# An attention block's opening on one core: the order of its first projections, loads and moments

## The reference

```python
xn = layernorm(x)                                   # no scale, no shift, eps 1e-5
kqv = xn @ Wqkv + bqkv                              # 768 columns: q, k, v
scores = einsum('bsnh,btnh->bnst', k, q) / 4
scores = triu(scores) + -10000.0 * tril(ones, k=-1)
attn = softmax(scores, axis=2)                      # over s: down the columns
out = einsum('bnkq,bknh->bqnh', attn, v).reshape(b, s, 256) @ Wo + bo
xq = fp8(clip(xn / in_scale, -448, 448)) * in_scale
return x + out + einsum('bsi,oi->bso', xq, weight * weight_scale)
```

## Time and profile before

| | |
|---|---|
| median of 3 runs | 200.75 us (199.69 to 200.75) |
| the profiled execution | 200.16 us, of which the span is 198.1 us |
| TensorE busy in the span | 175.9 us (89%) |
| VectorE | 161.9 us (82%) |
| GpSimd | 122.8 us (62%) |
| ScalarE | 98.3 us (50%) |
| TensorE's granted clock, mean | 0.955 of full |

### The profile page before, as it was taken

One profiled execution on the slowest core, in us unless ns is written; L12 is line 12 of the kernel. 1 busy time (PEld: TensorE's weight loads), 2 busy tenths in 40 slices (PEclk: granted clock), 3 DMA queues, 4 the chain that ended last, 5 costly groups with the idle time before them and its releaser, 6 DMA issues.

```text
span 198.1 us, 4702 instructions
## 1 busy us (share of the span) xinstructions
PE 175.9 (89%) x1677; PEld 137.6 (69%) x1677; DVE 161.9 (82%) x344; ACT 98.3 (50%) x169; POOL 122.8 (62%) x245
## 2 busy tenths in 40 slices
PE   4597648399989999999999999999999987999992
PEld 4476446278667878787878787878787866776661
DVE  2889989986988899889988998899889987891441
ACT  2614230156546753774377447644664464549410
POOL 7720704415996599459945994599459956666600
PEclk9969966759999999999999999999999999999999
DMA  5799999702530371137113541362126210001003
GB/s 168 180 345 184 234 190 232 132 0 72 144 110 3 95 203 35 55 92 196 45 56 87 135 109 58 87 175 72 56 77 173 81 53 2 6 1 58 0 3 106
DMA packets 23673, 20.35 MB, mean 103 GB/s; under 512 B 2547, under 2 KB 23395, under 8 KB 23651
## 3 DMA queue, kind: packets, MB, share of 16 engines
q1 hardware_dynamic: 23651, 20.06, 40.6%
HBM read 3.48 MB, written 2.10 MB: 28 GB/s over the span
## 4 chain that ended last, share of the span: by engine, by line
PE 73%; DMA 9%; DVE 5%; SPq 4%; POOL 3%; ACT 2%; issue 2%; ACTq 0%
PE pso L1002 8%; PE bankB L1027 8%; PE ps L977 8%; PE bankA L1089 6%; PE bankB L1035 5%; PE bankA L1027 5%; DMA k_stack<-k_parts 4%; SPq L358 4%; PE pso L1008 4%; PE ps L954 3%; PE ps L956 3%; DMA q_stack<-max_rows 3%; PE ps L949 3%; PE ps L982 3%; PE bankB L1056 2%; PE bankA L1074 2%
## 5 line engine op out<-in xcount | busy, mean ns | idle before, releaser
L462 POOL TENSOR_SCALAR_AFFINE_SELECT probs<-probs 128x256 f32<-128x256 f32 x128 | 54.5, 455 | 40.2 <-ACT probs L532 40.0
L743 DVE TENSOR_REDUCE row_max<-ps 128x4 f32<-128x1024 f32 (+1 forms) x48 | 58.2, 1216 | 10.4 <-PE ps L956 9.6
L532 ACT ACTIVATE probs<-ps 128x1024 f32<-128x1024 f32 x48 | 48.9, 1023 | 29.9 <-PE ps L977 23.7
L954 PE MATMUL ps<-k_stack,q_stack 96*128 96x128 bf16 x128 | 19.4, 229 | 2.0 <-DVE row_max L743 2.0
L977 PE MATMUL ps<-q_stack,k_stack 99*128 99x256 bf16 x128 | 20.0, 282 | 0.6 <-DMA q_stack<-max_rows 0.6
L956 PE MATMUL ps<-k_stack,q_stack 125*128 125x128 bf16 x128 | 19.4, 228 | 0.0
L1027 PE MATMUL bankB<-xT,wqk_sb 128*128 128x256 f32 x64 | 17.6, 422 | 1.4 <-ACT xT L582 1.4
L1002 PE MATMUL pso<-probs,v_sb 128*32 128x256 f32 x256 | 17.5, 386 | 0.0
L556 ACT ACTIVATE o_raw<-pso 128x512 f32<-128x512 f32 x16 | 9.6, 597 | 15.9 <-PE pso L1008 15.9
L949 PE MATMUL ps<-k_stack,q_stack 125*128 125x128 bf16 x128 | 11.1, 236 | 6.7 <-DMA k_stack<-k_parts 3.9
L472 POOL TENSOR_TENSOR x_sum<-x_clip,x_big 128x256 f32<-128x256 f32 x16 | 11.3, 723 | 7.3 <-DVE x_big L732 7.3
(11 more groups left out here) (130 smaller groups left out, 347.7 us busy)
## 6 DMA issues: line engine op xcount, KB each, us to landing
q_stack<-q_parts SPq DMA_DIRECT2D x48, 128.0 KB
k_stack<-k_parts SPq DMA_DIRECT2D x48, 128.0 KB
out_dram<-y SPq DMA_DIRECT2D x8, 256.0 KB, 2.1
x_all<-in_L_attn_x_dram SPq DMA_DIRECT2D x1, 1536.0 KB, 8.8
k_stack<-fixed_k SPq DMA_DIRECT2D x3, 256.0 KB
q_stack<-fixed_q SPq DMA_DIRECT2D x3, 256.0 KB
x_all<-in_L_attn_x_dram SPq DMA_DIRECT2D x2, 256.0 KB, 2.8
wqkv_sb<-in_L_attn_Wqkv_dram SPq DMA_DIRECT2D x1, 512.0 KB, 3.8
```

The lines of the kernel that those rows point to most:

```text
L462: ins = pool.affine_select(out=v[:, lo:lo + 2], in_=v[:, lo:lo + 2], compare_op=ALU.is_ge, fill=0.0, base=0, pattern=[[0, 2], [1, P]], cha ...
L532: act.activation(probs[:, i, :], ps[:], ACT.Exp, scale=SCALE).then_inc(exp_done, 1)
L743: dve.tensor_reduce(dst, src, AX_X, ALU.max).then_inc(max_done, 1)
L954: pe.matmul(ps[:, h * S:h * S + P], q_stack[0:PROD, b % STACKS, hh, P:S], k_stack[0:PROD, b % STACKS, hh, 0:P], start=True, stop=True)
```

## The change

1. **Loads.** x comes in four groups: batch 0, batch 1, batches 2 and 3, batches 4 to 7. The last group, `bo` and `wo` are issued behind stack 0's pieces.
2. **Fixed rows of stack 1.** No DMA writes them: ScalarE copies q's (four copies, two on either side of xT of batch 1), GpSimd copies k's (four copies, behind its split of batch 1). TensorE waits for both ahead of phase 1 of batch 1, and `stack_full` counts two DMAs fewer for that stack.
3. **ScalarE's order.** Root 1 is taken behind both first parts of batch 0 instead of ahead of them. In step FIRST the copy of the maxima's rows comes first, then the moments of tiles 10 to 15, root 3, and only then the floor's exponential.
4. **VectorE's order.** Ones are filled into v here instead of on GpSimd. Batch 1's root and normalising go behind q's split; moments and variances of group 2 and the clipping of batch 0's x come ahead of batch 1's rests, its magnitude between them. The fp8 weight, the copy of v's bias, the row numbers and masked keys move in between the first maxima. The moments of two tiles and the variances of group 3 (tiles 8 to 15, six of them with ScalarE's sums) end step FIRST; their reciprocal root is in step 1.
5. **TensorE's order.** The transposes of v's bias and of the fp8 weight move from behind v's product to behind the second block of phase 1, the bias product from behind the second to behind the fourth. The warm-up is 13 products instead of 18 transposes.

```diff
-        WARM_UP = 18
+        WARM_UP = 13
-        X_GROUPS = ((0, TB), (TB, 2 * TB), (2 * TB, B * TB))
+        X_GROUPS = ((0, TB), (TB, 2 * TB), (2 * TB, 4 * TB), (4 * TB, B * TB))
@@ sync
             load_x(2)
-            sp.dma_start(bo_all[:], bo.partition_broadcast(P)).then_inc(proj_landed, 16)
-            sp.dma_start(wo_sb[:], wo.rearrange("(k p) n -> p k n", p=P)).then_inc(proj_landed, 16)
...
             to_stack(0)
-            fixed_in_stack(1)
+            sp.dma_start(bo_all[:], bo.partition_broadcast(P)).then_inc(proj_landed, 16)
+            sp.dma_start(wo_sb[:], wo.rearrange("(k p) n -> p k n", p=P)).then_inc(proj_landed, 16)
+            load_x(3)
             to_stack(1)
@@ gpsimd
-            pool.memset(v_sb[:], 1.0).then_inc(v_ones_ready, 1)
...
+            pool.wait_ge(split_ready, 4)
+            for h in range(0, H, 4):
+                ins = pool.tensor_copy(k_stack[ROW_MAX:ROW_MAX + FIXED_ROWS, 1, h:h + 4],
+                                       fixed_k[:].rearrange("r t p -> r (t p)").unsqueeze(1).to_broadcast([FIXED_ROWS, 4, S]))
+            ins.then_inc(fixed_k_copied, 1)
+            pool.wait_ge(fixed_k_copied, 1)
             round_x(0, 0)
@@ scalar
+            def copy_fixed_q(lo, hi):
+                for h in range(lo, hi, 4):
+                    ins = act.activation(q_stack[ROW_MAX:ROW_MAX + FIXED_ROWS, 1, h:h + 4],
+                                         fixed_q[:].rearrange("r t p -> r (t p)").unsqueeze(1).to_broadcast([FIXED_ROWS, 4, S]),
+                                         ACT.Copy)
+                return ins
...
+            def moments():
+                act.wait_ge(x_landed[3], 16)
+                for t in range(*ACT_TILES):
+                    ins = act.activation(act_out[:, t - ACT_TILES[0]], x_all[:, t, :], ACT.Copy, scale=-1.0 / D,
+                                         accum_out=act_mean[:, t:t + 1])
+                ins.then_inc(act_means, 1)
+                act.wait_ge(act_means, 1)
+                for t in range(*ACT_TILES):
+                    ins = act.activation(act_out[:, t - ACT_TILES[0]], x_all[:, t, :], ACT.Square, bias=act_mean[:, t:t + 1],
+                                         accum_out=act_sum[:, t:t + 1])
+                ins.then_inc(act_squares, 1)
...
-                if st.has(1):
+                if st.like == FIRST:
+                    rows_out(0, 0, "B")
+                    moments()
+                    square_roots(3)
+                    floor_out(0, 0, 0)
+                elif st.has(1):
                     max_out(n + 1, 1 - p, 0, "B")
...
-            for b in range(2):
-                xT_out(b, b)
-                if b == 0:
-                    square_roots(1)
-                    act.wait_ge(bqk_col_ready, 1)
-                part1(b, b, "q", "B")
-                part1(b, b, "k", "A")
+            xT_out(0, 0)
+            act.wait_ge(bqk_col_ready, 1)
+            part1(0, 0, "q", "B")
+            part1(0, 0, "k", "A")
+            square_roots(1)
+            act.wait_ge(const_ready, 2)
+            copy_fixed_q(0, HALF)
+            xT_out(1, 1)
+            copy_fixed_q(HALF, H).then_inc(fixed_q_copied, 1)
+            part1(1, 1, "q", "B")
+            part1(1, 1, "k", "A")
@@ vector, opening (new order)
+            dve.memset(v_sb[:], 1.0).then_inc(v_ones_ready, 1)
...
+            inverse_std(0)
+            normalise(0, 0)
...
+            link(moments(*X_GROUPS[1]))
+            variances(1)
...
             rest1(0, 0, "q", "B")
             split(dve, 0, 0, "q")
+            inverse_std(1)
+            normalise(1, 1)
             rest1(0, 0, "k", "A")
             split(dve, 0, 0, "k")
             dve.wait_ge(x_landed[2], 16)
-            moments(at, at + 5)
+            link(moments(*X_GROUPS[2]))
+            variances(2)
+            clip_x(0, 0)
             rest1(1, 1, "q", "B")
-            moments(at + 5, at + 8)
+            magnitude_x(0, 0)
             rest1(1, 1, "k", "A")
@@ vector, step FIRST
                     maxima(st, n + 1, 0)
+                if st.like == FIRST:
+                    fp8_weight()
...
                 if st.like == FIRST:
-                    inverse_std(2)
+                    dve.wait_ge(x_landed[3], 16)
+                    link(moments(X_GROUPS[3][0], ACT_TILES[0]))
                     normalise(2, 0)
+                    variances(3)
@@ tensor
             for _ in range(WARM_UP):
-                pe.transpose(ps1[:, 0:P], ident[:], ident[:])
+                pe.matmul(ps1[:, 0:P], ident[:], ident[:], start=True, stop=True)
...
                         if st.like == FIRST and i == 1:
+                            transpose_weights()
+                        if st.like == FIRST and i == 3:
                             bias_product()
```

More of the change, by code:

```diff
@@ L53 @@
 PARTS = 3
+ACT_TILES = (5 * TB, B * TB)
 Q_ROWS = (0, 0, 1, 0, 1, 2)
@@ L235, in build @@
         bank = {"A": psum("bankA", [P, 512]), "B": psum("bankB", [P, 512])}
-        x_landed = [sem(f"x{g}_landed") for g in range(3)]
+        x_landed = [sem(f"x{g}_landed") for g in range(4)]
         w_landed, bqk_landed, ffn_landed = sem("w_landed"), sem("bqk_landed"), sem("ffn_landed")
@@ L511, in _ @@
                 split(pool, 1, 1, qk)
+            pool.wait_ge(split_ready, 4)
[4 more added lines that the diff above has]
+            pool.wait_ge(fixed_k_copied, 1)
             round_x(0, 0)
             pool.wait_ge(out_bias_ready, 1)
-            for g in range(3):
-                pool.wait_ge(x_landed[g], 16)
+            pool.wait_ge(x_landed[0], 16)
+            pool.wait_ge(x_landed[1], 16)
             residual(0)
@@ L571, in max_out, with rows_out @@
                                scale=SCALE).then_inc(e_ready, 1)
+            def rows_out(b, half, bk):
+                c = 2 * b + half
                 act.wait_ge(max_mm, c + 1)
@@ L576, in max_out @@
                                ACT.Copy).then_inc(max_rows_ready, 1)
+            def max_out(b, par, half, bk):
+                floor_out(b, par, half)
+                rows_out(b, half, bk)
+            def moments():
[9 more added lines that the diff above has]
+                ins.then_inc(act_squares, 1)
             def xT_out(b, par):
@@ L669, in moments, with aggregate, from_act @@
                 return ins
+            def aggregate(lo, hi):
+                for t in range(lo, hi):
+                    ins = dve.bn_aggr(mean_var[:, t, :], stats[:, t, :])
+                return ins
+            def from_act(lo, hi):
+                dve.wait_ge(act_squares, 1)
+                dve.tensor_scalar(mean_var[:, lo:hi, 0], act_mean[:, lo:hi], -1.0, None, ALU.mult)
+                link(dve.tensor_scalar(mean_var[:, lo:hi, 1], act_sum[:, lo:hi], 1.0 / D, None, ALU.mult))
             def variances(g):
                 lo, hi = X_GROUPS[g]
-                for t in range(lo, hi):
-                    ins = dve.bn_aggr(mean_var[:, t, :], stats[:, t, :])
-                link(ins)
+                if g < 3:
+                    link(aggregate(lo, hi))
+                else:
+                    link(aggregate(lo, ACT_TILES[0]))
+                    from_act(*ACT_TILES)
                 dve.tensor_scalar(var_eps[:, lo:hi], mean_var[:, lo:hi, 1], EPS, None, ALU.add).then_inc(init_dve, 1)
@@ L842, in run @@
                     negate_and_split(n + 1, 0)
+                if st.like == FIRST:
+                    dve.wait_ge(w8_mm, 1)
+                    dve.tensor_copy(w8T[:], pso[:, 1, 1].bitcast(BF16).rearrange("p (k o) -> p k o", k=KT)).then_inc(w8T_ready, 1)
+                    link(dve.tensor_reduce(row_number[:], later[:], AX_X, ALU.add))
+                    for t in range(TB):
+                        ins = dve.tensor_scalar(masked_keys[:, t:t + 1], row_number[:], -1.0, float(S - 1 - P * t), ALU.mult, ALU.add)
+                    link(ins)
                 if st.has(-1):
@@ L897, in _ @@
             dve.wait_ge(x_landed[2], 16)
-            moments(at, at + 5)
+            link(moments(*X_GROUPS[2]))
+            variances(2)
+            clip_x(0, 0)
             rest1(1, 1, "q", "B")
-            moments(at + 5, at + 8)
+            magnitude_x(0, 0)
             rest1(1, 1, "k", "A")
-            fp8_weight()
-            dve.wait_ge(bias_mm, 1)
-            dve.tensor_copy(bv_T[:], pso[:, 0, 0].rearrange("p (k m) -> p k m", k=KT)).then_inc(bv_T_ready, 1)
-            link(moments(at + 8, last))
-            variances(2)
             dve.wait_ge(const_ready, CONSTS)
-            link(dve.tensor_reduce(row_number[:], later[:], AX_X, ALU.add))
-            for t in range(TB):
-                ins = dve.tensor_scalar(masked_keys[:, t:t + 1], row_number[:], -1.0, float(S - 1 - P * t), ALU.mult, ALU.add)
-            link(ins)
             dve.wait_ge(floor_ready, 1)
-            clip_x(0, 0)
             all_steps(dve, run)
@@ L1101, in transpose_max_early, with transpose_weights @@
                 mm.then_inc(max_mm, 1)
```

(18 more changed lines are left out.)

47 lines of the change are left out of this document (27 added, 20 removed).

## The result

The changed kernel takes 205.68 us (median of 4 runs, 204.74 to 205.76), the kernel before 200.74 us beside it (199.69 to 200.75): a ratio of 1.0197, 95% interval 1.0145 to 1.0248. It is slower by 4.9 us, outside the range.

A forecast was written before the change was run, and what follows sets the result against it. The opening, before 58 us, was taken as the bound: q at half clock, DMA backlog, VectorE's maxima, ScalarE's exponential. Gains and additions nearly cancel: 200.16 + 0.1 = 200.3, or 200.8 on the median's base; 200.4 given, range 198.2 to 203.3.

The forecast's parts named there:

- Part 1: Warm-up, q and k of batch 0: 13 products keep the clock up, so q's products end at 11.4 instead of 13.1.
- Part 2: Batch 0's stack: without the 4 us DMA backlog, issues end at 20.1 and it lands at 22.5 instead of 27.6.
- Part 3: Batch 1's normalising and products, v of batch 0: first maximum at 25.5 against 28.78, a gain of 3.3 us.
- Part 4: VectorE between the maxima: additions lengthen its full line by 2.9 us, bounds 2.2 and 3.8; step 0's first maximum at 39.7.
- Part 5: ScalarE's last root and table load: first large exponential 0.6 us later, at 41.4; batch 2's q products at 43.7, +0.1 us.
- rival D: ScalarE's sums come later than VectorE asks for them: +1.5 us, 201.9; chance 0.08.
- the five cases: The prediction's outcomes for the whole time: 200.4 (chance 0.38), 198.8 (0.29), 202.4 (0.20), 201.9 (0.08), 201.7 (0.05).
- B: Faster: batch 1's products at full clock, VectorE's additions only 2.2 us; 198.8, down to 197.8; chance 0.29.
- C: Slower: clock falls before batch 0's q products all the same; first maximum later than 26.5; 202.4, up to 203.7; chance 0.20.
- my two signs of being wrong: TensorE's clock up between 36 and 44 us, or the first maximum later than 27.

## Why the prediction was wrong

**Part 1 holds.** The warm-up is 26 records, q takes 1.96 us (1.99 forecast), and its first part starts at 11.46. The clock stayed up with 0.63 us without work ahead of q.

**Part 2 holds.** SP's last pieces were issued from 18.15 to 20.04 (20.1), and neither the first scores nor step 0's first, at 40.82, wait for a DMA.

**Part 3 named what is late next, and was 1.1 us short.** Batch 1's normalising ended at 16.2 (16.3). The doubt about three microseconds without work was right, but I gave it four microseconds at half clock; it lasted 6.8, from 16.4 to 23.2, over the transposes, all of q and half of k. The first maximum came at 26.60, not 25.5. Filling the gap gave 1.55 of that back.

**Part 4 was mis-sized: +4.0 us for +2.9, beyond its upper bound of 3.8.** By starts of neighbouring rows, the weight took 1.67 us (27.74 to 29.41), taken at about 1.25. The larger miss is a term that I didn't have: the second group's reciprocal root takes 2.02 us (36.69 to 38.71), 0.92 more than before. The output's bias now stands directly ahead of it, with no maximum between, so GpSimd's residual, which waits for that bias, runs beside the small operations:

```profile
36.85 1.40 POOL L489 TENSOR_TENSOR xb<-x_all,out_bias 128x256 f32<-128x256 f32 x2 [1.50 <-DVE out_bias L934]
```

rstd_sq and rstd_e take 0.70 and 0.65 us there, 0.21 and 0.17 before, each as long as one of GpSimd's two. Of this the Trainium skill's page "SBUF — State Buffer" (SBUF: two separate sides) says that VectorE and GpSimd share a pair of ports as an exclusive lock, which binds a VectorE operation with two inputs in SBUF while GpSimd reads it. By that rule it is the two products that are held, and for them the trace agrees. The reciprocal ahead of them (0.17 us) is no test: it ended at 36.86, as GpSimd began.

**Part 5: ScalarE was priced well, TensorE's clock was left out.** Load and root came 1.77 us behind the maximum to the exponential (1.7 forecast), and ScalarE's sums ended at 40.13 (37.3 forecast) before VectorE asked at 41.5, so rival D is out too. They began 2.1 us later than I put them (34.56 for 32.5) and took 5.6 us for 4.8, as twelve reads of the accumulator at 0.18 us were not in it; only VectorE's own delay hid that. The step that failed is "q's products start at 43.7": I placed them at the instant at which the clock came back in the profile before, and took this instant as fixed. In the profile it came back 6.9 us later, at 50.6, and step 0 paid 2.9 us, by the kernel with dummies. I had even written that the clock was at half "when the maxima had left TensorE little to do", and used that only for batch 1's products. None of the five cases had the clock low behind 43.7.

That TensorE's idle stretches between the maxima matter is shown: dummies in two of them (1.12 and 3.99 us long) keep the clock up. That they alone set the instant of its return isn't. Here TensorE stands empty again for 0.46 us ahead of 43.19 and 0.52 us ahead of 44.75, where in the kernel before it had work without a break from 39.77. But in the kernel before with the new warm-up it had work without a break from 37.54, and the clock came back at 46.5. In six profiles of the changed kernel and its variants without these dummies it came back between 49.0 and 52.0; of the kernel before there is one profile. So the long dip belongs to the changed kernel as far as these can say, and the 43.6 may in part be the luck of one execution.

**Step 1's five small operations** were "nothing, at most 0.5 us" and cost 1.0 in steps 1 and 2 together. VectorE's 18.38 of 20 us busy said that 1.6 us were free on average, not that they were free ahead of the last maxima.

**The sum again.** From the forecast of +0.1: the exponential 2.3 us later (part 3's 1.1, part 4's 1.1, part 5's 0.1), of which 0.8 doesn't reach the next copy (in the kernel with dummies the exponential is 2.3 late and that copy, at 62.95, 1.5 later than the forecast's 61.44; it has the full clock from 36 us on, which the kernel before lacked until 43.6, so this isn't TensorE's slack alone); 2.9 for the clock in step 0; 1.0 for steps 1 and 2. That makes 0.1 + 2.3 − 0.8 + 2.9 + 1.0 = 5.5, the difference of the spans.

**The rivals.** B needed the clock up through batch 1's products and was wrong on it. C's point, a first maximum later than 26.5, was met at 26.60, but not by its mechanism. The case that happened, a longer last dip, was none of them. Neither of my two signs of being wrong came either: the clock was low from 36.9 to 44 us, as I had said, and the first maximum was ahead of 27. Both looked at the time before 44 us only.

What stays open: what decides, from run to run, in which places the clock falls and when it comes back. The runs show the price of three dips (1.5 us at batch 1's products, 2.9 in step 0, 1.2 to 1.7 in step 6), not their timing; that of the fall near 30 us was not measured.

## What to carry to other kernels

Where an engine's clock depends on its load, an edit that makes the opening faster can also make the gaps in it wider (3.16 us ahead of batch 1's transposes for 0.39 before): price each stretch of the new order at the clock it would then have, and never take the instant at which the clock came back as given. If TensorE has idle stretches on the way to its full part, try dummy products into a free bank there; here the same reordering was 2.0% slower without them and, with small work moved out of the full engine's line, 0.7% faster. In the kernel before, dummies in one place changed nothing that the time could show. And before small operations are put behind an edit, look at what GpSimd starts on the result of the row ahead of them.

## What was not expected of the hardware

- An accumulating operation on ScalarE brings a second instruction of 0.18 us, and a tile's sum comes every 0.40 us (mean) or 0.49 us (squares).
- Behind a table load of 1.28 us the next operation starts 0.01 us later (43.55 to 43.56), and it begins 0.02 us after the root. The Trainium skill's page "ScalarE: Activation LUTs" (What ACT_TABLE_LOAD costs) adds 1.38 us of drain to the load; no run here shows it, and the measurement decides.
- Ahead of the first fall of the clock in a profile, the granted clock in the rows is no evidence. In the changed kernel with the old warm-up it reads 1.00 for 8 to 16 us, while the four transposes at 8.00 took 1.12 us and q 3.75, as at half clock.
- A dip of TensorE's clock in one place moved the end of the same later work by up to 1.7 us (56.4 to 58.1 us from the last copy), in kernels whose code there is the same; spans of single executions therefore compare only with the clock's strip beside them.
